# Decoder layer on one core: the last two rounds' tokens in 23 groups of 128 rows, residual and results in 512 KB pieces

## The reference

```python
gate_scores = softmax(x @ Wg + bg)                 # 8 experts
h = relu(einsum('btc,ech->bteh', x, W1) + b1)      # 128 -> 512
expert_out = einsum('bteh,ehc->btec', h, W2) + b2  # 512 -> 128
topk_scores, topk_idx = top_k(gate_scores, 2)
top_probs = softmax(topk_scores)
out = sum(take(expert_out, topk_idx) * top_probs)
```

## Time and profile before

| | |
|---|---|
| median of 3 runs | 1040.76 us |
| lowest, highest | 1035.5, 1041.91 us |
| profiled execution, its own time | 1042.74 us |
| its span in the trace | 1040.9 us |
| granted TensorE clock, mean | 0.865 |
| busy: PE, DVE, POOL, ACT | 76%, 71%, 68%, 47% |
| SP's DMAs, share of the 16 DMA engines | 43.9% |

### The profile page before, as it was taken

The page is one execution under the profiler, slowest core; times in us unless marked ns, Lnnn a source line. Parts: engine busy times, 40 slices in busy tenths (PEclk is TensorE's granted clock), DMA queues, the critical chain, the costliest instruction groups (busy, mean ns, idle before and its releaser), DMA issues. The chain is left out here.

```text
span 1040.9 us, 12598 instructions
## 1 busy us (share of the span) xinstructions
PE 787.0 (76%) x3871; PEld 498.4 (48%) x3871; DVE 744.2 (71%) x1060; ACT 488.9 (47%) x1086; POOL 704.4 (68%) x501
## 2 busy tenths in 40 slices
PE   5667677797778778867877886774768998799592
PEld 1233343363344345334524542452446688798592
DVE  3279987989996897899789889958952625233172
ACT  3557456557475545746564674434213334232130
POOL 0159987978699779878977996787661445554252
PEclk9888788998899679878976997776688999999797
DMA  2324382282264228225522642385016446867872
GB/s 67 126 101 147 125 246 95 93 214 84 91 179 139 84 96 225 90 91 149 167 84 83 190 127 75 121 202 162 1 37 194 132 116 178 255 187 196 270 215 79
DMA packets 111076, 143.51 MB, mean 138 GB/s; under 512 B 18392, under 2 KB 83557, under 8 KB 111008
## 3 DMA queue, kind: packets, MB, share of 16 engines
q1 hardware_dynamic: 106016, 134.26, 43.9%
q0 software_dynamic: 4992, 8.45, 2.5%
HBM read 110.48 MB, written 34.01 MB: 139 GB/s over the span
## 5 line engine op out<-in xcount | busy, mean ns | idle before, releaser
L1185 POOL TENSOR_TENSOR prod<-hst,BC 128x1024 f32<-128x1024 f32 x128 | 303.9, 2374 | 121.6 <-DVE hst L1332 120.3
L1332 DVE TENSOR_TENSOR_SCAN hst<-dA,Rp 128x1024 f32<-128x1024 f32 x128 | 292.6, 2286 | 12.2 <-DVE Rp L1323 0.4
L993 ACT ACTIVATE dA<-dtm,Aneg 128x255 f32<-128x255 f32 x512 | 216.0, 495 | 146.4 <-DVE hst L1332 146.2
L571 PE MATMUL Y<-prod,ident 128*128 128x256 f32 x512 | 167.7, 461 | 65.0 <-POOL prod L1190 58.6
L1266 POOL DMA_INDIRECT y2d<-prod,BC x92 | 90.6, 984 | 136.6 <-DVE prod L1627 114.9
L571 PEld LDWEIGHTS Y<-prod,ident 128*128 128x128 f32 x512 | 108.5, 225 | 140.7 <-POOL prod L1190 93.8
L1190 POOL TENSOR_TENSOR prod<-prod 128x512 f32<-128x512 f32 x128 | 163.6, 1278 | 10.0
L1323 DVE TENSOR_TENSOR Rp<-BC,Rp 128x1024 f32<-128x1024 f32 x128 | 156.5, 1223 | 5.5 <-DMA BC<-bcd 1.5
L571 PE MATMUL Rp<-BC,prod 128*128 128x128 f32 x736 | 92.0, 279 | 8.2 <-DVE prod L1627 8.2
L571 PE MATMUL T<-Kbd,qT 64*128 64x512 f32 x128 | 62.5, 862 | 45.9 <-DVE mx L1376 45.9
L571 PEld LDWEIGHTS Rp<-BC,prod 128*128 128x128 f32 x736 | 90.5, 195 | 13.3 <-issue 10.8
(11 more groups left out here) (222 smaller groups left out, 1255.7 us busy)
## 6 DMA issues: line engine op xcount, KB each, us to landing
BC<-bcd SPq DMA_DIRECT2D x64, 1024.0 KB, 5.4
BC<-in_L_ffn_W SPq DMA_DIRECT2D x92, 256.0 KB
xsd<-blank SPq DMA_DIRECT2D x18, 1032.0 KB, 13.8
BC<-xsd SPq DMA_DIRECT2D x46, 129.0 KB
soft<-in_L_ffn_b SPq DMA_DIRECT2D x46, 64.0 KB
xin<-in_x SPq DMA_DIRECT2D x8, 256.0 KB, 4.1
x2d<-x2o SPq DMA_DIRECT2D x8, 256.0 KB
E<-x2d SPq DMA_DIRECT2D x1, 2048.0 KB
```

The source lines that it names most:

```text
L571: return pe.matmul(o, l, r_, start=start, stop=stop, **kw)
L993: m = A(dA[:, k % RING, i, 1:SEQ], dtm[:, r % 2, d, b * SEQ + 1:(b + 1) * SEQ], ACT.Exp, scale=Aneg[:, d, c * NC + i:c * NC + i + 1])
L1185: TT(prod[:, k % RING, :, :], hst[:, k % RING, :, :], BC[:, (k // 2) % BCR, 1, :, :], ALU.mult).then_inc(s_pd, 1)
L1332: v.tensor_tensor_scan(hst[:, k % RING].rearrange("p n s -> p (n s)"), dA[:, k % RING].rearrange("p n s -> p (n s)"), U.rearrange("p n s - ...
```

## The change

Part 1 gets groups of 128 rows: `Part` has a new argument `tall` (tiles in a group), 2 for part 0 and 1 for part 1. Part 1 then has 2 * 1024 / 128 + 7 = 23 groups (31 to 53) in place of 15. Everything that a group of part 1 does has half the rows: one transpose, four up matmuls of 128 columns, four down matmuls, one scatter. Its five loads stay, the rows' one with half the bytes.

The residual is loaded in four DMAs of 512 KB, after the loads of groups 21, 24, 27 and 30, each with a semaphore of its own, and the next group's load no longer waits for the last x2 to be stored. The six early loads of results come one by one, after the loads of groups 36 to 41.

The eight scatters of a round all come in the slots k = 13, 14, 15 (two, three and three of them). Before, there was one each in the slots 13, 14, 15 and in 0 to 4 of the next round. The tail slots of round 10 fall away.

```diff
+    def __init__(self, first, last, base, group, tall):
+        self.first, self.last, self.base, self.group, self.tall = first, last, base, group, tall
         self.region = (last - first) * TOK
-        self.most = self.region // GROUP
-        self.groups = 2 * self.region // GROUP + EXPERTS - 1
+        self.rows = tall * P
+        self.most = self.region // self.rows
+        self.groups = 2 * self.region // self.rows + EXPERTS - 1
...
+PARTS = [Part(0, SPLIT, 0, 0, GT)]
+PARTS.append(Part(SPLIT, ROUNDS, EXPERTS * PARTS[0].region + SPARE, PARTS[0].groups, 1))
...
+def tall_of(j):
+    return PARTS[0 if j < PARTS[1].group else 1].tall
+
+
+def sent(i, last):
+    return 16 * sum(tall_of(j) for j in range(i, last + 1, YR))
...
-        LASTS = 2 * STEPS + 5
+        LASTS = 2 * STEPS
...
                 if j >= XR:
-                    sp.wait_ge(s_y[(j - XR) % YR], 16 * GT * ((j - XR) // YR + 1))
-                sp.dma_start(xr[:, n, :, :].rearrange("p i c -> p (i c)"),
-                             xsd[bass.ds(row, GROUP), :].rearrange("(p i) c -> p (i c)", i=GT)).then_inc(s_xr[n], 16)
+                    sp.wait_ge(s_y[(j - XR) % YR], sent((j - XR) % YR, j - XR))
+                sp.dma_start(xr[:, n, 0:part.tall, :].rearrange("p i c -> p (i c)"),
+                             xsd[bass.ds(row, part.rows), :].rearrange("(p i) c -> p (i c)", i=part.tall)).then_inc(s_xr[n], 16)
...
+            def load_residual(i):
+                n = ROUNDS // FINAL
+                if i == 0:
+                    sp.wait_ge(Tp.sem, Tp.at("o", ROUNDS - 1))
+                sp.wait_ge(s_x2, 16 * n * (i + 1))
+                sp.dma_start(acc[:, i * n * NTT:(i + 1) * n * NTT, :].rearrange("p (r t) c -> p r (t c)", t=NTT),
+                             x2d[i * n:(i + 1) * n, :, :, :].rearrange("r p t c -> p r (t c)")).then_inc(s_acc[i], 16)
...
                 if j == 3 * WR:
                     store_x2(ROUNDS - 1)
-                    sp.wait_ge(s_x2, 16 * ROUNDS)
-                    sp.wait_ge(Tp.sem, Tp.at("o", ROUNDS - 1))
-                    sp.dma_start(acc.rearrange("p (r t) c -> p r (t c)", t=NTT), x2d[:, :, :, :].rearrange("r p t c -> p r (t c)")).then_inc(s_acc, 16)
+                if j > 3 * WR and j % 3 == 0 and j // 3 - WR <= FINAL:
+                    load_residual(j // 3 - WR - 1)
...
-                if j == PARTS[1].group + WR - 1:
+                n = j - PARTS[1].group - WR + 1
+                if n == 0:
                     scattered(PARTS[1].group)
-                    for i in range(early):
-                        load_results(i)
+                if 0 <= n < 2 * early:
+                    load_results(*divmod(n, 2))
...
-                for i in range(GT):
+                for i in range(tall_of(j)):
                     m = pe.transpose(Turned[:, i * P:(i + 1) * P], xr[:, j % XR, i, 0:D], ident[:, :])
...
-                        m = mm(Up[j % 2][half][:, i, :], w1r[:, j % WR, c * P:(c + 1) * P], xg[:, j % 2, :])
+                        m = mm(Up[j % 2][half][:, i, 0:tall_of(j) * P], w1r[:, j % WR, c * P:(c + 1) * P], xg[:, j % 2, 0:tall_of(j) * P])
...
-                if tail2 and k < 2 * NTT - 3:
-                    scatter(r - 3, k + 3)
                 if tail:
                     if k == 9:
                         row_ids(r - 2)
                     if k >= STEPS - 3:
-                        scatter(r - 2, k - STEPS + 3)
+                        for n in ((0, 1), (2, 3, 4), (5, 6, 7))[k - STEPS + 3]:
+                            scatter(r - 2, n)
```

More of the change, by code:

```diff
@@ L332, in decoder @@
         s_ys = sem("s_ys")
-        s_acc = sem("s_acc")
+        s_acc = [sem(f"s_acc{i}") for i in range(FINAL)]
         s_y = [sem(f"s_y{i}") for i in range(YR)]
@@ L409, in behind @@
         def behind(r):
-            return 1 <= r <= ROUNDS, 2 <= r <= ROUNDS + 1, 3 <= r <= ROUNDS + 2
+            return 1 <= r <= ROUNDS, 2 <= r <= ROUNDS + 1
         TRIO = ((0, 1), (4, 5)), ((2, 3), (6, 7))
@@ L506, in load_group @@
                 row = sp.value_load(table[0:1, 0, j:j + 1], min_val=part.base,
-                                    max_val=part.base + EXPERTS * part.region + SPARE - GROUP)
+                                    max_val=part.base + EXPERTS * part.region + SPARE - part.rows)
                 e = sp.value_load(table[0:1, 1, j:j + 1], min_val=0, max_val=EXPERTS - 1)
@@ L532, in scattered @@
                 for i in range(YR):
-                    sp.wait_ge(s_y[i], 16 * GT * len(range(i, groups, YR)))
+                    sp.wait_ge(s_y[i], sent(i, groups - 1))
             sp.wait_ge(s_pd, ROUNDS * STEPS)
@@ L561, in _ @@
             for i in range(early, FINAL):
-                load_results(i)
+                for c in range(2):
+                    load_results(i, c)
             for i in range(early, FINAL):
@@ L759, in slot @@
                 ln, nxt = ahead(r)
-                prev, tail, tail2 = behind(r)
+                prev, tail = behind(r)
                 if tail:
@@ L1142, in tile_in @@
                     act.wait_ge(s_ub, j - 1)
-                A(xg[:, j % 2, :], Turned, ACT.Copy).then_inc(s_xg, 1)
+                A(xg[:, j % 2, 0:tall_of(j) * P], Turned[:, 0:tall_of(j) * P], ACT.Copy).then_inc(s_xg, 1)
             def tile_relu(j):
@@ L1598, in group_table @@
                 then(v.tensor_tensor(tiles[:, :], pos[:, (part.last - 1) % 2, NTT, :], first[:, i, :], ALU.subtract))
-                then(v.tensor_scalar(tiles[:, :], tiles[:, :], 1.0 / GROUP, None, ALU.mult))
+                then(v.tensor_scalar(tiles[:, :], tiles[:, :], 1.0 / part.rows, None, ALU.mult))
                 then(v.tensor_tensor(ov, tiles[:, :].unsqueeze(2).to_broadcast(each),
@@ L1609, in group_table @@
                 then(v.tensor_tensor(start[:, 0:n], countf[:, 0:n], start[:, 0:n], ALU.subtract))
-                then(v.tensor_scalar(start[:, 0:n], start[:, 0:n], float(GROUP), float(part.base), ALU.mult, ALU.add))
+                then(v.tensor_scalar(start[:, 0:n], start[:, 0:n], float(part.rows), float(part.base), ALU.mult, ALU.add))
                 then(v.scalar_tensor_tensor(table[:, 0, at], expert[:, 0:n], float(part.region), start[:, 0:n], ALU.mult, ALU.add))
@@ L1642, in results @@
                     v.wait_ge(s_e[i], 32)
+                    v.wait_ge(s_acc[i], 16)
                 for t in range(i * n, (i + 1) * n):
```

20 lines of the change are left out of this document (7 added, 13 removed).

## The result

The changed kernel took 1093.67 us (median of 4 runs, 1085.94 to 1097.39) beside 1041.03 us for the kernel before on the same chip (1035.5 to 1041.91): 1.0508 times, with an interval of 1.0433 to 1.0583. It is 53 us slower where 27 were forecast, and outside the forecast's range.

The account below looks back on a forecast made before the run. PE was taken to bound the group stage, with SP's load issuing equally slow and next to bind. 1042.74 + 10.9 - 3 + 27.6 - 6.6 - 1.2 = 1070.4, less 2.0 against the median: 1068 us, range 1050 to 1081.

Parts of the forecast that it names:

- the residual in pieces: Group loads from group 19 on: no wait for the last x2, no 2 MB between loads; 0 to 10 us won, -3 taken.
- Scatters in the scan: Scan stage: two more scatters ahead of the gate delay it 2.46 us in five rounds, 12.3 us, less 1.4: +10.9.
- PE's wait near 4 us and DVE's for x1T over 5: Sign for the scan stage: PE's wait for the later gate near 4 us, DVE's for x1T over 5.
- the upper bound (15 us): Scan stage: PE's sum of step 15, behind three more scatters, delays the attention; at most one scatter more a round, 15 us.
- The saved gate (-1.4): End of the scan stage: the gate (1.41 us) now comes after all eight scatters, before the first group load: -1.4 us.
- absorbed: Rival, scan stage: POOL's extra 2.46 us vanish in DVE's slack, giving 1056 us; chance 0.15.
- The 6 us that it worked out from the Trainium skill: Residual load: three more DMAs at about 2 us fixed each, 6 us; not in the sum, 1074 if waited for.
- Part 1's pace: Loads of groups 31 to 53: SP's issuing sets 22 intervals of 3.95 us, plus 5.4 for result loads; +27.6.
- PE's work sets the pace: Rival, part 1: SP's interval falls with group size, so PE's halved work decides; some 1028 us; chance 0.06.
- transfers: Rival, part 1: weight and result transfers hold up the loads, interval 4.5 us, 12 us more, 1080 us; chance 0.14.
- The end: Last load to last output: 10.5 us in place of 17.1, -6.6, and one scatter less, -1.2.

Follow-up runs that it names:

- e3: Kernel before with only the residual and result loads in pieces (256-row groups, old scatters): 1035.17 us, 0.9922 times the kernel before.
- e1: Kernel before with the scatters alone moved to slots 13, 14, 15 (two, three, three): 1066.67 us, 1.0246 times the kernel before.
- e2: Kernel before with 128-row groups in the last 23 groups alone: 1064.88 us, 1.0189 times the kernel before.
- e4: Changed kernel with the scatters put back where they were: 1061.58 us, 1.0195 times the kernel before.
- e14: Changed kernel, unchanged, run again on chip E: 1069.72 us, 1.0332 times the kernel before.
- e16: Changed kernel, unchanged, run a third time, on chip F: 1072.18 us, 1.0354 times the kernel before.
- e11: Changed kernel with old scatter places and without the two bias loads in each of the last 23 groups: 1028.83 us, 0.9957 times the kernel before.
- e7: Changed kernel with a short POOL memset after each scatter of rounds 6 and 7 and each store of groups 0 to 30: 1092.49 us, 1.0503.
- e6: Changed kernel with the scatters of rounds 6 and 7 spread to one a slot again: 1078.31 us, 1.0369 times the kernel before.
- e8: Changed kernel with a long POOL memset (128x1024) after each scatter of rounds 6 and 7 and each store of groups 0 to 30: 1093.92 us, 1.0518.
- e5: Kernel before with the scatters of rounds 0 to 5 alone in bursts: 1057.30 us, 1.0180 times the kernel before.
- e9: The placed version: kernel before with loads in pieces and scatters moved into POOL's idle slots, 256-row groups: 1009.44 us, 0.9755 times the kernel before.

## Why the prediction was wrong

On chip A it failed in the step "the residual in pieces": -3 stood there for the whole of groups 0 to 31, and +19.6 was measured. The pieces did neither good nor harm that can be told (e3: 0 to 31 in 166.4 us, as on the same chip in e1, e2 and e4, within 2.4 us). The scatters of rounds 6 and 7 lie in that piece, and the step gave them only the 6.2 us for which they hold POOL, hidden behind the rest. Two things were shown:

- **The dense scatters cost a little there without any remote wait.** 0 to 31 takes 159.7 and 160.2 us with them (e14, e16), 156.6 without (e11, on another chip): +3 to 4.
- **In the runs on chips A, B and C the stage is longer for every kernel, and on A and C more so with dense scatters.** The kernel before takes 163.8 us there, against 155.3 on E; the changed one 183.3 (A) and, with the filler that changes nothing, 181.1 (C), against 159.7 and 160.2 on E and F. What is added, 8.5 us and 21 to 24 us, goes with waits called remote, and on C 17 us of it went when the scatters were spread (181.1 to 164.2, e7 and e6). So about 15 of the 19.6 us come from an effect that, on A and C, took both: dense scatters and such a chip (or time). Of the 23.6 us between A and E, 8 are PE's own busy time in that piece (156.3 against 148.3 us): its granted clock in it was 0.91 on A, 0.54 just behind a standstill, and 0.98 on E. Chip B fits less well: in e1, with dense scatters on 256 rows, the stage took 166.9 us, no more than without them (e2). That execution was e1's fastest, 1059.59 us where the median is 1066.67, so it may show less of the effect than the others had.

What this effect is stays open. On chip C a DMA every 2.1 us had none and one every 1.3 us had it; on D, E and F one every 1.3 us had none. That PE's signals are late is what the traces show. In the nine traces of A to C that have remote waits, 14 to 18 of PE's semaphore updates come over 1 us after the recorded end of their matmul, up to 11.1 us, all of them in the stage of groups (the resets at the program's end are left out); in e8 none does, and in the ten traces of D to F none is more than 0.1 us late. What holds the signals isn't in them. That the spread and the placed versions are free of it on a chip like A wasn't seen either, since chips D to F don't have it. The prediction had seen such a wait (7.18 us) and put it down to the 2 MB transfer because it fell into it. That was the error of reading: other waits with the same name (4.98 us at 833.36, 2.32 at 880.97) end before the load was issued at 883.97, and were not looked at.

**By chip E**, where both kernels were profiled and no signal is late, the terms stand so: to load 0 +14.8 (forecast +10.9), 0 to 31 +4.4 (-3), part 1 +28.0 (+27.6), the end -8.9 (-7.8). The sum is +38.4 for these executions, +35.2 between medians, +38.0 on chip F, where +27 was forecast. So even without the effect the forecast was 8 to 11 us low, mostly in groups 0 to 31 (7 us) and in the scan (4 us).

**Scatters in the scan.** POOL's stretch grew nearly as forecast (from 33.1 to 35.8 us, 2.6 where 2.46 was taken), but the wait that was to pass the delay on is gone, and +15.4 us were measured for +10.9. A scatter in a row costs 1.27 us (0.97 and 0.30 of issue), not 1.23; four of the five gates slipped by 2.73 to 2.77 us, and one, of round 6, by 4.55. "PE's wait near 4 us and DVE's for x1T over 5" was wrong: the wait at x1T fell to 6.8 us in total, and oT's 18.2 us came. PE waits for no gate any more: the path was the attention's, behind the fold of step 15, which the text had as the upper bound (15 us). Behind three of the five gates x1T still comes 2.1 us after the gate's end, as before: there the attention's delay happens to be as long as the gate's, which is luck. Behind round 5's it comes 3.9 us after it, and so round 6's gate is the one that slipped by 4.55. The saved gate (-1.4) can't be told apart. The rival "absorbed" is refuted by e5. e9 shows from the other side that scatters in POOL's stretch cost: six of them out of it make it 6.4 us shorter.

**Residual in pieces.** -3 was to come from group 19 on, and e3 shows none of it; its gain of 8 us comes from the results behind group 36, and with 128-row groups there is none. The text also counted four more issues for four pieces in place of one, which is three. The 6 us that it worked out from the Trainium skill (page "DMA: Bandwidth & Descriptors", section "Anatomy of one DMA") rest on a fit that the page gives for DMAs issued by GpSimd; SP issues these, and no trace has a wait put down to the residual's load.

**Part 1's pace.** Right, in mechanism and size: 3.93 us (3.95 taken), the whole piece 90.5 (92.3). e11 shows the cause. The rival "PE's work sets the pace" would have needed an interval of 2.7: SP comes near that only with three DMAs in place of five (2.68 to 2.88). Its 1028 us is 2 too high besides: 1040.8 - 23 + 10.9 - 3 is 1026. The rival "transfers" is refuted, the DMA share was 0.75 at 3.93 us.

**The end.** Right: -6.2 and -8.9 for -7.8. The last output ends 12.1 us after the last load (10.6 on chip E), where 10.5 was taken.

## What to carry to other kernels

When work is cut into smaller pieces, look first at who issues its transfers: five small DMAs for each group cost one queue 3.7 to 3.9 us, with 128 rows as with 256, and the engine that got half the work only waited. An engine that works without a gap ahead of a wait that others share should get its extra instructions elsewhere: the same eight scatters cost 15 us in a burst there and gave 17 back when they went into the slots in which POOL idled. A wait with a name that one can't explain should be followed through all its occurrences before it is blamed on what happens beside it, and a difference that rests on such waits should be measured on a second chip.

## What the runs showed of the hardware

- The same two kernels stood at 1.0508 on one chip and, later, at 1.0332 and 1.0354 on two others. The excess lies in waits of DVE and ACT of up to 10 us, called remote, while POOL issues indirect DMAs 1.27 us apart. They end when PE's semaphores are raised, up to 11 us after the recorded ends of the matmuls and several within 0.2 us of each other; on the other chips these signals are never over 0.1 us late.
- An indirect DMA of 128 rows takes POOL 0.97 us and 0.30 us until the next; a short memset (0.17 us) between two of them fits into that time.
- An issue less saves SP 0.53 us: 3.93 us a group with five, 2.88 with three (3.75 and 2.68 where nothing holds it up).
